# Attention of a decoder layer in two passes: maxima of all heads first, then transposed scores whose exponentials feed the values' products

## The reference, cut to what matters

```
x = x + attention(layernorm(x))                      # 16 heads of 32, 2 key/value heads, RoPE, causal
x = x + state_space(ctx, gate=layernorm(x))          # conv, 16 states, scan along the sequence
x = x + ffn(layernorm(x))                            # 1408 wide, top-2 of 8 low-rank adapters

scores = einsum('bhgqd,bhkd->bhgqk', q, k) * scale   # attention, the part that changes
scores = where(causal, scores, -inf)
attn   = softmax(scores, axis=-1)
out    = einsum('bhgqk,bhkd->bhgqd', attn, v)
return out.reshape(...) @ wo.T
```

## Time and profile before

| | us |
|---|---|
| median of 3 runs (1648.47 to 1651.48) | 1651.27 |
| the profiled execution | 1649.75 |
| its span, first to last instruction | 1647.9 |
| PE, DVE, ACT busy | 1406.0, 1218.4, 604.9 |
| mean granted TensorE clock | 0.876 |

### The profile page before, as it was taken

The page is one execution under the profiler, slowest core; times in us unless marked ns, Lnnn a source line. Parts: engine busy times, 40 slices in busy tenths (PEclk is TensorE's granted clock), DMA queues, the critical chain, the costliest instruction groups (busy, mean ns, idle before and its releaser), DMA issues.

```text
span 1647.9 us, 16148 instructions
## 1 busy us (share of the span) xinstructions
PE 1406.0 (85%) x5768; PEld 685.0 (42%) x5768; DVE 1218.4 (74%) x1411; ACT 604.9 (37%) x1436; POOL 111.9 (7%) x116
## 2 busy tenths in 40 slices
PE   5756767999888799899889699899879788799999
PEld 2333433443333354444334255444334345454434
DVE  4899996589989766759998865759998967623330
ACT  5165553323223584232232376242333267211110
POOL 0000001001100000000110000100210000100000
PEclk8855558999999699899999779899999869789999
DMA  4167761123666631112656822012556741101112
GB/s 185 39 147 153 154 141 27 44 66 108 143 141 166 166 66 26 39 50 78 159 128 159 196 68 52 26 37 84 124 131 152 173 135 27 26 13 64 48 32 83
DMA packets 53278, 158.81 MB, mean 96 GB/s; under 512 B 5072, under 2 KB 10704, under 8 KB 44752
## 3 DMA queue, kind: packets, MB, share of 16 engines
q0 software_dynamic: 9216, 67.11, 19.8%
q1 hardware_dynamic: 25664, 54.23, 9.9%
q10 hardware_dynamic: 18320, 36.45, 8.6%
HBM read 86.20 MB, written 4.46 MB: 55 GB/s over the span
## 4 chain that ended last, share of the span: by engine, by line
DVE 30%; issue 30%; PE 29%; DMA 6%; ACT 4%; POOL 2%; DVEq 0%; ACTq 0%; POOLq 0%
DVE state L1091 11%; DMA y_sb<-state 5%; PE ps_a L894 5%; DVE state L1086 4%; PE ps_a L974 4%; PE ps_a L820 3%; DVE state L1096 3%; PE ps_b L834 3%; PE ps_w L873 3%; PE ps_a L906 3%; POOL rstd L477 2%; PE ps_b L914 2%; PE ps_w L782 2%; ACT r L625 2%; DVE neg_max L1126 2%
## 5 line engine op out<-in xcount | busy, mean ns | idle before, releaser
L894 PE MATMUL ps_a<-xt,w_sb 128*128 128x512 f32 x704 | 319.2, 607 | 0.0
L1091 DVE TENSOR_TENSOR_SCAN state<-decay,state 128x2048 f32<-128x2048 f32 x64 | 282.8, 4418 | 5.3 <-ACT decay L583 0.5
L677 ACT ACTIVATE r<-ps_a 128x512 f32<-128x512 f32 x132 | 78.6, 596 | 380.6 <-PE ps_a L906 202.8
L894 PEld LDWEIGHTS ps_a<-xt,w_sb 128*128 128x128 f32 x704 | 138.1, 197 | 174.9 <-issue 174.9
L820 PE MATMUL ps_a<-r 32*128 32x512 f32 (+3 forms) x512 | 140.4, 634 | 81.7 <-ACT r L625 55.2
L906 PE MATMUL ps_a<-r,wb_sb 128*128 128x512 f32 x352 | 177.1, 628 | 35.9 <-DVE r L1267 33.7
L583 ACT ACTIVATE decay<-dt_sb,decay_rate 128x511 f32<-128x511 f32 x256 | 162.9, 712 | 104.9 <-DVE state L1096 72.2
L1260 DVE SCALAR_TENSOR_TENSOR r<-r,ps_a 128x512 f32<-128x512 f32 x132 | 89.9, 681 | 146.3 <-ACT r L677 146.3
L625 ACT ACTIVATE r<-ps_a,neg_max 128x128 f32<-128x128 f32 (+3 forms) x256 | 133.6, 534 | 116.6 <-DVE neg_max L1126 116.1
L974 PE MATMUL ps_a<-wd_sb,r 128*128 128x512 f32 x352 | 162.4, 613 | 0.0
L1086 DVE TENSOR_TENSOR state<-du_sb,bc_sb 128x2048 f32<-128x2048 f32 x64 | 146.3, 2286 | 4.7 <-DMA y_sb<-state 4.6
(11 more groups left out here) (120 smaller groups left out, 1475.7 us busy)
## 6 DMA issues: line engine op xcount, KB each, us to landing
y_sb<-state POOLq DMA_DIRECT2D x64, 1024.0 KB, 9.7
bc_sb<-bc_rows ACTq DMA_DIRECT2D x64, 512.0 KB, 5.1
w_sb<-in_w_tiles SPq DMA_DIRECT2D x44, 512.0 KB, 3.7
wd_sb<-in_w_down SPq DMA_DIRECT2D x44, 256.0 KB, 3.5
wb_sb<-in_w_adapt SPq DMA_DIRECT2D x44, 128.0 KB, 2.1
xa<-in_x SPq DMA_DIRECT2D x4, 1024.0 KB, 5.2
out_x<-xb SPq DMA_DIRECT2D x16, 256.0 KB, 7.0
xn_att<-in_ctx_t SPq DMA_DIRECT2D x4, 512.0 KB, 6.1
```

The source lines that it names most:

```text
L894: mm = nc.tensor.matmul(ps_a[:, 2 * (f % 2) + half, :], w_sb[:, slot, at + k * P:at + (k + 1) * P], xt[:, k, :], start=(k == 0), stop=Fals ...
L1091: nc.vector.tensor_tensor_scan(flat, decay[:, n % 2, :, :].rearrange("p j l -> p (j l)"), flat, 0.0, ALU.mult, ALU.add).then_inc(scan_chai ...
```

## The change

The attention of a batch is done in two passes over 16 groups (4 query tiles m times 4 blocks) of four heads.

- *Pass 1* (`scores`, `maxima`): for every group the scores of 128 queries against the keys, masked, and their negated row maxima. Groups go from the widest query block to the narrowest. The results of all heads gather in `neg_max`. PE transposes that once (`turn_maxima`) and ACT copies it to `max_rows`.
- *Pass 2* (`weights`, `weigh_values`): for every group the scores with 128 keys on the partitions and up to 512 queries along the row, the transposed mask, and a product that adds the queries' negated maxima; ACT takes the exponentials of two heads at once; they feed the values' products directly, and a product with `ones` gathers the row sums of all 16 heads in one bank.
- *At the end* DVE inverts the sums (two reciprocals of 128x256), PE spreads them, DVE scales everything (two products of 128x1024), and then come all four `project_out`. Three `project_in` of the next batch now stand among these, ahead of `project_out`, and their ACT part too.
- *Moved:* query tiles 1 to 3 are projected and rotated inside pass 1 instead of beside the down products.
- *Tables:* no scan piece stands in pass 1. `PLAN_FIRST` keeps 13 pieces beside the projections and has 47 in pass 2; `PLAN_NEXT` has 13 instead of 22 beside the down products and 17 in pass 2, none behind the last two groups.
- *Gone:* transposes and copies of the probabilities, row sums by ACT, 32 small inversions and 16 spreads per batch.

```diff
-IN_DOWN = 22 
+IN_DOWN = 13
+IN_MAXIMA = 0
 FREE_DOWN = 1
-LAST_STEPS = 1
+LAST_STEPS = 2
...
 def between(free, used):
+    if used >= ATT:
+        return max(free + 1, used - 2)
...
+def late_tile(g):
+    m, _, k = group(g)
+    return (m + 2, k) if m + 1 < MT and k < 3 else (None, None)
+def pair_of(u):
+    return u % 3
...
+        def score_banks(u):
+            if pair_of(u) < 2:
+                return ps_a[:, 2 * pair_of(u):2 * pair_of(u) + 2, :]
+            return ps_b[:] if u < STEPS else ps_w[:]
+        sums, values = ps_b[:, 0, :], ps_b[:, 1, :]
...
             # ACT, attention
+                for n in range(GROUPS):
+                    exponents(n)
+                    if n > 0 and n % NT == 0:
+                        move_values(n // NT - 1)
+                    load_bc(b, slots[ATT + GROUPS + n])
+                    make_decay(b, slots[ATT + GROUPS + n])
...
             # PE, attention
+                def scores(g):
+                    m, i, k = group(g)
+                    if k == 0:
+                        pe.wait_ge(qk_ready, b * TILES + m + 2)
+                    if g == 0 and not first_batch(b):
+                        pe.wait_ge(x3_ready, b * NT)
...
+                    if 2 * g + 1 >= 3:
+                        pe.wait_ge(neg_max_ready, b * STEPS + 2 * g - 1)
...
+                for g in range(GROUPS):
+                    n, k = late_tile(g)
+                    if k in (0, 1):
+                        project_raw(b, n, range(2 * k, 2 * k + 2))
+                    if k == 2:
+                        rotate_raw(b, n)
+                    scores(g)
...
+                def weights(n):
+                    m, kt = n // NT, n % NT
+                    width = L - kt * P
...
                     for j in range(HPT):
+                        nc.tensor.matmul(score_banks(STEPS + 2 * n + j // 2)[:, j % 2, 0:width],
+                                         k_t[head_rows(j), kt * P:(kt + 1) * P], q_t[head_rows(j), m, kt * P:L],
+                                         start=True, stop=False, tile_position=(j * HD, 0))
...
+                    for j in range(HPT):
+                        pick = ident[head_rows(j), j * HD + m:j * HD + m + 1].to_broadcast([HD, P])
+                        mm = nc.tensor.matmul(score_banks(STEPS + 2 * n + j // 2)[:, j % 2, 0:width],
+                                              pick, max_rows[head_rows(j), kt * P:L],
+                                              start=False, stop=True, tile_position=(j * HD, 0))
...
+                turn_maxima()
+                weights(0)
+                for n in range(GROUPS):
+                    if n + 1 < GROUPS:
+                        weights(n + 1)
+                    weigh_values(n)
+                pe.wait_ge(exp_done, (b + 1) * STEPS)
+                for half in range(2):
+                    if b + 1 < BATCH:
+                        project_in(b + 1, [half])
+                    spread_inverse(half)
+                if b + 1 < BATCH:
+                    project_in(b + 1, range(2, XIN_EARLY))
+                for i in range(NT):
+                    project_out(b, i)
...
             # DVE, attention
+                for g in range(GROUPS):
+                    n, k = late_tile(g)
+                    if k == 2:
+                        rotate_tile(b, n)
+                    maxima(g)
+                    for piece in slots[ATT + g]["dve"]:
+                        scan_piece(b, piece)
+                for n in range(GROUPS):
+                    for piece in slots[ATT + GROUPS + n]["dve"]:
+                        scan_piece(b, piece)
+                dve.wait_ge(pv_done, (b + 1) * GROUPS)
+                invert(0)
+                invert(1)
+                dve.wait_ge(pv_moved, (b + 1) * MT)
+                divide(0)
+                divide(1)
+                for i in range(NT + 2):
+                    gate_stages(i)
```

More of the change, by code:

```diff
@@ L167, in uses_of @@
             names += [("xin", j) for j in range(XIN_EARLY)]
+        names += [("op", i) for i in range(NT)]
         names += [("yt", i) for i in range(NT)]
@@ L375, in use @@
                 k, before = USES_LAST[name], len(USES_FIRST) + (BATCH - 1) * len(USES_NEXT)
-            elif not ffn and isinstance(b, int) and b == 0:
+            elif not ffn and b == 0:
                 k, before = USES_FIRST[name], 0
@@ L630, in move_transposed @@
[L630 to L636, removed]
-                        nc.scalar.activation(probs_t[(2 * s + k) % 8][:, 0:(i + 1) * P],
-                                             ps_b[:, k, 0:(i + 1) * P], ACT.Copy).then_inc(pt_ready, 1)
@@ new lines, in attention, with exponents @@
+                act.wait_ge(max_turned, b + 1)
+                nc.scalar.activation(max_rows, values, ACT.Copy).then_inc(max_moved, 1)
+                def exponents(n):
+                    kt = n % NT
+                    width = L - kt * P
+                    for p in range(2):
+                        act.wait_ge(weights_full, b * STEPS + 2 * n + p + 1)
+                        if n >= 2 and p == 0:
+                            act.wait_ge(pv_done, b * GROUPS + n - 1)
+                        nc.scalar.activation(probs_t[n % 2][:, 2 * p:2 * p + 2, 0:width],
+                                             score_banks(STEPS + 2 * n + p)[:, :, 0:width], ACT.Exp)\
+                            .then_inc(exp_done, 1)
@@ new lines, in weigh_values @@
+                def weigh_values(n):
+                    m, kt = n // NT, n % NT
+                    width = L - kt * P
+                    pe.wait_ge(exp_done, b * STEPS + 2 * n + 2)
+                    if kt == 0 and m > 0:
+                        pe.wait_ge(pv_moved, b * MT + m)
+                    for j in range(HPT):
+                        mm = nc.tensor.matmul(values[head_rows(j), kt * P:L], v_sb[:, kt, j // 2 * HD:(j // 2 + 1) * HD],
+                                              probs_t[n % 2][:, j, 0:width], start=(kt == 0), stop=(kt == NT - 1),
+                                              tile_position=(0, j * HD), skip_group_check=True)
+                    if kt == NT - 1:
+                        mm.then_inc(pv_full, 1)
+                    for j in range(HPT):
+                        mm = nc.tensor.matmul(sums[head_rows(j), kt * P:L], ones[:, m, :],
+                                              probs_t[n % 2][:, j, 0:width], start=(n == 0), stop=(n == GROUPS - 1),
+                                              tile_position=(0, j * HD), skip_group_check=True)
+                    mm.then_inc(pv_done, 1)
@@ L996, in _ @@
             for t in range(BATCH - 1):
-                project_in(t + 1, range(XIN_EARLY))
                 transpose_gated(t)
```

355 lines of the change are left out of this document (171 added, 184 removed).

## The result

The changed kernel takes 1690.64 us, median of 4 runs (1688.55 to 1695.17); the kernel before, 1651.38 (1648.47 to 1652.43). The ratio is 1.0244, 95% interval [1.0217, 1.0271]: slower by 39 us, where 34 were forecast.

| | before | after | difference | forecast |
|---|---|---|---|---|
| end of batch 0's | 269.8 | 295.4 | +25.6 | +31 |
| to that of batch 1, 2, 3 | 383.6, 385.0, 385.4 | 392.7, 392.0, 389.0 | +9.1, +7.0, +3.6 | +1 each |
| from there to the end | 224.1 | 224.2 | +0.1 | 0 |

A forecast was written before the change was run, and what follows sets the result against it. DVE was taken to set the pace in batch 0's attention and before later batches' first scores. The profiled 1649.75 us + 31 for batch 0 + 3 x 1 for batches 1 to 3 = 1684, range 1632 to 1745.

The forecast's parts named there:

- +1 each: Batches 1 to 3: 26 us gained before the first scores, eaten by an attention of 127 us instead of 100.
- The sign and its cause: Whole kernel slower, chance 0.79; batch 0 costs +31 us, since pass 1 has no pieces and pass 2 all 47.
- The 50: Pass 1 of batch 0: 50 us, taken between 43 at full clock and 64 at half.
- The walk: Step-by-step timing of pass 1: 11.5 us per tile with late projection, 8.3 without; 43 us at full clock, 64 at half.
- The sum: Stage times added up per batch: batch 0 +31 us, batches 1 to 3 +1 each, 1684 us in all.
- not 26: Down products of batches 1 to 3: first scores at 527.3 instead of 553.5, a gain of 26 us per batch.
- not 45: Pass 1 of batches 1 to 3: 45 us, PE coming from dense work with a pause of 3 us.
- (1): Both passes at full speed: pass 1 35 us, -15 per later batch, batch 0 +14, kernel 1619 us; chance 0.19.
- (2): Clock stays at half in the attention: kernel 1773 us, or 1728 if it rises midway; chance 0.16.
- (3): Four heads' score strips don't run at once: 29 us more per later batch, kernel 1781 us; chance 0.08.
- (4): Down products not pulled ahead: 7 us less gain per batch, kernel 1705 us; chance 0.57 together with the main forecast.
- The other marks: Signs for the new profile, among them DVE idle about a quarter of pass 1 and four `project_out` in 14 us.

The follow-up runs named there:

- experiment 1: The changed kernel with 12 of batch 0's 47 scan pieces moved from pass 2 back into pass 1: 1677.29 us, ratio 1.0162 to the kernel before.
- experiment 2: The changed kernel with each addition to `y_sb` cut to the first half of its columns: 1657.69 us, ratio 1.0043 to the kernel before.
- Experiment 4: The changed kernel with three buffers of down weights (`wd_sb`) instead of two: 1673.07 us, ratio 1.0134 to the kernel before.
- experiment 3: The changed kernel with DVE's rotation of the next query tile put behind the group's maxima instead of ahead: 1669.64 us, ratio 1.0111 to the kernel before.
- experiment 5: The changed kernel with the next batch's `project_in` and ACT's moves of its tiles put behind `project_out`: 1684.47 us, ratio 1.0190 to the kernel before.

## Why the prediction was right, and where not

**The sign and its cause: right.** Batch 0 costs the most, for the reason given: DVE idles in pass 1, and 15 states follow at the additions' pace. Experiments 1 and 2 show both halves. By the steps: first maximum 73.1 (forecast 72.6); pass 1 44.4 us (50, the one that was off); from there to the last out 152.3 (152), a state each 9.8; the end 25.6 (26). The 50 was off by where it was put more than by its size. The walk starts with the first scores; these came at 68.8, and from there pass 1 took 48.7 us. The sum set the walk behind the first maximum, 4.3 us later. The clock was as mixed as the choice of 50 between 43 and 64 supposed: 0.79 on the mean, 0.50 in the last 11.4 us (106.1 to 117.5).

**"+1 each" for batches 1 to 3: mis-sized, it was +9.1, +7.0 and +3.6.** The total owes something to luck: batch 0 cost 5 us less than forecast and the later batches 17 more, and these errors partly cancel. For batch 1 the pieces are these.
- *Down products:* a gain of 23.3, not 26. The walk had DVE last, at 527; in fact PE was, after 5.0 us for down weights that the sum did not hold. The sum took the moved projections and rotations off PE's time as if nothing hung on them; but they stood between most tiles of down products, and the loads landed beside them. Experiment 4 takes back 4.3 us of it.
- *Pass 1:* 47.6, not 45. The rotation ahead of the maxima was in the walk at full clock; its pause slows what comes behind it too, which experiment 3 shows. The last tile ran at the lower level (granted clock 0.50 from 594.2 to 605.6) and took 11.1 us, near the walk's 11.4 at half clock, not 8.3.
- *Pass 2:* 57.8 to the end of the last out (forecast: 56, and 2 for the turning). DVE works through it but for 5.3 us of waits for `bc_sb` and `y_sb`.
- *The end:* 24.8 (24).
- *FFN:* from `project_out` to the next down products 200.1 for 197.9, where no change was forecast. In experiment 1, whose edit ends before this stage, it takes 196.8. So it varies by 3 us with nothing changed in it, and the 2.2 are not shown to come from the change. The granted clock of its first 48 us is 0.79 after, 0.86 in experiment 1 and 0.93 before; that it is the cause is not shown either. In the periods of batches 2 and 3 it was 0.3 and 1.0.

The shortfall of 2.7 in the gain, 3.1 more for the attention (130.1 for 127) and the 2.2 of the FFN, over the forecast's 1, make the 9. Batch 3 loses less, since its end holds no projection for a next batch: 22.0 us for 24.8.

**The rivals.** (1) fell as it stood: the attention took 130.1 us and not under 115, pass 1 taking 47.6 us for its 35 because the bank and queue waits do not overlap. It was the right place, though: with the rotation moved, pass 1 comes to 41.2 us (experiment 3). (2) fell for the attention as a whole: the granted clock was 0.81 and 0.98 in the two passes, so the lower level held for some 18 us of pass 1. (3) fell: 1.07 us for four strips of 512. The Trainium skill ("TensorE: Matmul & The Clock Gate", Part 3) would have made that an estimated 1.14; the trace gives 1.07, start to start as the prediction counts it (the row's own 1.14 runs into the masks'). (4) fell for the down products as a whole: 2.7 us of the gain were missing, not 7, and PE waited for weights, not for ACT or v.

**The other marks.** DVE idles 31% and 36% of pass 1, not a quarter. The `project_out` take 13.90 us in one row. The reciprocals cost 3.4 us, 1.7 each, inside bounds of 0.4 to 2.7: with PE's work beside them they cost `project_out` little, but the projection that was to hide them stood in its way (experiment 5).

## What to carry to other kernels

When a stage is split so that one engine only answers another, look for where the answering engine's long work goes: where it is full anyway (batch 0) spread that work over both parts, and where the other engine waits for each answer (later batches) keep pieces longer than the gaps out. In each queue, put the instruction that releases another engine ahead of the one that merely prepares; two lines in another order were worth 21 us here. Before taking work out from between two uses of a buffer, ask whether the buffer's next load fits in what is left: that work hid the load, and no wait in the rows of before told so.

## What the runs showed of the hardware

A reciprocal of 256 elements per partition takes longer on DVE than an elementwise product of 1024; from after's groups by shape (busy, mean ns | idle before):
```profile
L1202 DVE RECIPROCAL r<-ps_b 128x256 f32<-128x256 f32 x8 | 13.4, 1722 | 0.0
...
L1207 DVE TENSOR_TENSOR r<-r,ps_a 128x1024 f32<-128x1024 f32 x8 | 9.8, 1222 | 18.5 <-PE ps_a L916 18.5
```
Halving an addition to `y_sb` does not halve its time: 1024 KB land after 9.5 us at the median, 512 KB after 7.2. The rows of page part 6, of after and of experiment 2 (KB each, us to landing):
```profile
y_sb<-state POOLq DMA_DIRECT2D x64, 1024.0 KB, 9.5
```
```profile
y_sb<-state POOLq DMA_DIRECT2D x64, 512.0 KB, 7.2
```
And a pause of 2.54 us on TensorE cost more than itself: the granted clock fell to its lower level behind it, and the products there took 3.02 us instead of 1.94. With a pause of 0.67 (experiment 3) the clock stayed at 1.00 and they took 1.94 again.
